# One-hots by scalar comparisons, weighted one-hots on ScalarE, and chunks in pairs on TensorE in a graph kernel's first pass

## The chip, the cores and the metric

The kernel runs on one core of a Trainium2 chip. The metric is the device time of one execution in microseconds, the median of the timed runs.

## What is computed

A graph has 6250 nodes with 256 features (`x`) and 106250 edges (`src`, `dst`, `edge_weight`), sorted by destination. Four layers follow one another; each adds its result to `x` and takes a layer norm.

```python
# layer 0: attention over heads for the first 6250 edges (the gathers of x by src and dst)
x = layernorm(x + attention(x, src[:n], dst[:n], W0, attn_l, attn_r))
# layer 1: plain graph convolution
norm = d1[src] * d1[dst];            x = layernorm(x + segment_sum((x @ W1)[src] * norm, dst))
# layer 2: two weighted convolutions with self loops, bias and relu
norm = d2[row] * w * d2[col];        h = relu(segment_sum(norm * (x @ W2)[row], col) + b1)
                                     h = relu(segment_sum(norm * (h @ W3)[row], col) + b2);  x = layernorm(x + h)
# layer 3: convolution the other way round (sums over src), with self loops
vals = d3[src] * d3[dst];            x = layernorm(x + segment_sum(vals * (x @ W4.T)[dst], src))
```

## The kernel before

**Blocks and chunks.** The nodes are cut into NBK = 49 blocks of 128. The edges of a destination block stand in NC = 18 chunks of 128 edges (882 chunks in all). For one chunk GpSimd gathers 128 table rows from memory into a slot of `G` (7 slots, L1766), VectorE makes a 128x128 one-hot `M` of the destinations by a scalar comparison (4 buffers, `onehot`, L1041 without weights, L1043 with), and TensorE multiplies the two in f32 and adds up the block in PSUM (L1689). Pass one (layer 1) does this for all 882 chunks. In it ScalarE also writes the edge weight as a 257th column of the slot (`weight_column`, L1362), three chunks ahead.

**What is built behind pass one.** Passes two and three do the last ND = 17 blocks (32 to 48, called dense here) from a matrix of weights that lies ready in memory (`AW`), and pass four (layer 3) is a product with the whole adjacency matrix (`AT`). Both are built during pass one, one source block after another in the order `BORDER`, in which a dense one comes at every third place or so. A function `build_steps` gives each step a due time in chunks, PITCH = 17 chunks a block; `behind` hands each engine its own steps, and each engine does those of chunk k after its own part of chunk k. Every engine works strictly in its order.

**The steps of block i.** VectorE marks the cell of each edge (`cellhot`), TensorE counts ranks (`rank`, L1577 and L1579), VectorE picks the rank and makes slot numbers (`pick`, `pack`, `over`, `less`, `slots`, L1094 to L1114), multiplies the cell one-hots by what is carried (`load`, L1122 and L1123, into `OHP`), and compares all 18 columns of slot numbers with a table in one instruction (`place`, L1126, into `S`). TensorE moves the payload to its slot by 18 products (`permute`, L1589). ScalarE copies the outcome out of PSUM as bf16 (`cells`, L1372, into `clb`: source, destination, and for dense blocks three pieces of the weight). Then 26 positions are done in batches of CB = 2: VectorE compares destinations (`doh`, L1139) and sources (`soh`, L1140, 128x512) for two positions at once, and for dense blocks multiplies the first by the three weight pieces (`wdoh`, L1143). TensorE multiplies them (`pair`, L1601; `weigh`, L1612, six products a position). ScalarE copies each pair of positions out of PSUM (`keep`, L1379; `keepw`, L1386), and SyncE stores them.

**Waits around the change.** `place` makes the whole of `S` and needs all permutes of the block before to be done; `permute` waits for it and for `load`. `pairhot` waits for the cells and for the batch four back to be used. `weigh` waits for VectorE's `wdoh`. A chunk's product on TensorE waits for the gather, for `M` and for the weight column (`s_wc`); the gather waits for a slot (7 chunks back).

Of the kernel before, what the change touches and what calls it, by code (L numbers as in the profile page):

```python
# [43 lines left out]
FILL_B, FILL_C = 1840, 600  # L44
# [149 lines left out]
def build_steps():  # L194
# [27 lines left out]
    V_.append((PITCH * NBK, ("bad",)))  # L222
# [288 lines left out]
def program(nc, a, out):  # L511
# [5 lines left out]
    with ExitStack() as ctx:  # L517
# [75 lines left out]
        irep18 = sb("irep18", [P, P, NC], BF16)  # L593
        irep25 = sb("irep25", [P, NPR, NC], BF16)
        irepS, irepD = sb("irepS", [P, D, CB], BF16), sb("irepD", [P, P, CB], BF16)
# [3 lines left out]
        S = sb("S", [P, P, NC], BF16)  # L599
        soh = [sb(f"soh{i}", [P, D, CB], BF16) for i in range(NB)]  # L600
        doh = [sb(f"doh{i}", [P, P, CB], BF16) for i in range(NB)]
        atp = [sb(f"atp{i}", [P, 512], BF16) for i in range(4)]
        wdoh = [sb(f"wdoh{i}", [P, 3, P, CB], BF16) for i in range(NB)]
# [8 lines left out]
        slots, slotb = sb("slots", [P, NBK, NC]), [sb(f"slotb{i}", [P, NC], BF16) for i in range(2)]  # L612
        clb = [sb(f"clb{i}", [P, 5, NPOS], BF16) for i in range(2)]
# [39 lines left out]
        s_wg, s_kw, s_wc, s_dn, s_lo, s_hi = (sem(n_) for n_ in ("s_wg", "s_kw", "s_wc", "s_dn", "s_lo", "s_hi"))  # L653
# [86 lines left out]
        def vector(e):  # L740
# [316 lines left out]
            def behind_(step):  # L1057
# [17 lines left out]
                elif kind == "cellhot":  # L1075
                    O_ = OH[j]
                    if i == 0:
                        w.wait_ge(s_io, 8)
                        w.wait_ge(s_ev, project_of(1, NBK - 1) + 1)
                        after("cell", "pay1", "dsum", "d1")  # L1080
# [27 lines left out]
                elif kind == "slots":  # L1108
                    if i >= 2:
                        after(("place", i - 2))  # L1110
                    done(e.scalar_tensor_tensor(out=slots[:, b, :], in0=OH[j][:, own + 1, :], scalar=-128.0, in1=slot0[:, :],
                                                op0=ALU.mult, op1=ALU.add), ("slots", i))
                    after(("slots", i))
                    done(e.tensor_copy(slotb[j][:, :], slots[:, b, :]), ("slotb", i))  # L1114
# [9 lines left out]
                elif kind == "place":  # L1124
                    after(("slotb", i))
                    done(e.tensor_tensor(S[:, :, :], irep18[:, :, :], slotb[j][:, :].unsqueeze(1).to_broadcast([P, P, NC]),  # L1126
                                         ALU.is_equal), ("place", i))
                elif kind == "pairhot":
# [3 lines left out]
                    value = lambda q, m_: clb[j][:, q, j0:j0 + g].unsqueeze(1).to_broadcast([P, m_, g])  # L1132
# [6 lines left out]
                    done(e.tensor_tensor(doh[n_ % NB][:, :, 0:g], irepD[:, :, 0:g], value(1, P), ALU.is_equal), ("doh", n_))  # L1139
                    done(e.tensor_tensor(soh[n_ % NB][:, :, 0:g], irepS[:, :, 0:g], value(0, D), ALU.is_equal), ("pairhot", n_))  # L1140
                    if b >= NB0:
                        after(("doh", n_))
                        done(e.tensor_tensor(wdoh[n_ % NB][:, :, :, 0:g], doh[n_ % NB][:, :, 0:g].unsqueeze(1).to_broadcast([P, 3, P, g]),  # L1143
                                             clb[j][:, 2:5, j0:j0 + g].unsqueeze(2).to_broadcast([P, 3, P, g]), ALU.mult), ("weighted", n_))
                elif kind == "bad":
                    after(("place", NBK - 1))
# [15 lines left out]
                elif kind == "deg":  # L1162
                    if b == 0:
                        w.wait_ge(s_io, 9)
# [90 lines left out]
        def scalar(e):  # L1255
# [108 lines left out]
            def behind_(step):  # L1364
                if step[0] == "cells":
# [3 lines left out]
                    if i >= 2:  # L1369
                        n_ = NBT * (i - 1) - 1  # L1370
                        w.wait_ge(s_v, max(at["pairhot", n_], at.get(("weighted", n_), 0)))
                    e.copy(clb[i % 2][:, 0:q_, :].rearrange("p k t -> p (k t)"), PC[:, 0:q_ * NPOS]).then_inc(s_ce, 1)  # L1372
# [73 lines left out]
        def tensor(e):  # L1446
# [115 lines left out]
            def behind_(step):  # L1562
# [20 lines left out]
                elif kind == "permute":  # L1583
                    c = step[2]
                    q_ = 5 if b >= NB0 else 2
                    w.wait_ge(s_v, at["place", i])
                    w.wait_ge(s_v, at["load", i])
                    w.wait_ge(s_ce, i)
                    e.matmul(PC[:, 0:q_ * NPOS], S[:, :, c], OHP[:, 0:q_, :, c], start=c == 0, stop=c == NC - 1).then_inc(s_pm, 1)  # L1589
                elif kind == "pair":  # L1590
# [5 lines left out]
                    d_, s_ = doh[n_ % NB][:, :, q], soh[n_ % NB][:, :, q]  # L1596
# [6 lines left out]
                elif kind == "weigh":  # L1603
# [4 lines left out]
                    w.wait_ge(s_v, at["weighted", n_])  # L1608
                    fill_free(w, "keepw", i, pair // 2)
                    for h in range(2):  # L1610
                        for t in range(3):
                            ins = e.matmul(ps[:, h * P:(h + 1) * P], soh[n_ % NB][:, h * P:(h + 1) * P, q], wdoh[n_ % NB][:, t, :, q],  # L1612
# [49 lines left out]
            def aggregate(p):  # L1662
                other = behind(p, 2)
                end = chunks_of(p)
                for k in range(end):
# [24 lines left out]
                    for step in other[k]:  # L1690
                        behind_(step)
                    for step in due(FOLLOW[p][2], k, end):
                        follow(p, step)
# [31 lines left out]
        def gpsimd(e):  # L1725
# [27 lines left out]
            io(irep18[:, :, :], [[1, P], [0, NC]])  # L1753
            io(irepS[:, :, :], [[1, D], [0, CB]])
# [163 lines left out]
```

## Time and profile before

| | us |
|---|---|
| median of 3 timed runs (3676.34 to 3695.49) | 3684.63 |
| the profiled execution, its own time | 3691.6 |
| its span | 3689.8 |

The profile is of one execution. Its page gives for each engine the time in which it was busy: PE is TensorE, DVE VectorE, ACT ScalarE, POOL GpSimd. Pass one runs from 294.8 us (first `M`) to about 1572 us, pass two to about 2340, pass three to about 3118, pass four to the end. A group of instructions is shown as busy time, mean ns of one, and the idle time of its engine just before them with what ended it. Instructions of one engine overlap a little, so a mean is somewhat longer than the distance from one start to the next.

### The profile page before, as it was taken

The page shows a single profiled execution, that of the slowest core. Times are in us where ns is not written, and L with a number is a line of the kernel's source. Part 1 is how long each engine was busy: PE and PEld are TensorE (multiplying, and loading weights), DVE is VectorE, ACT ScalarE, POOL GpSimd, SP SyncE. Part 2 cuts the span into 40 slices and gives each one's busy share as a digit, 9 for nine tenths or more (in the row PEclk, how much of TensorE's full clock was granted, in tenths as well). Part 3 has the DMA queues.
Part 4 walks back from the last instruction along what each step waited for, and adds up shares of the span by engine and source line. Part 5 has one row for each costly group of instructions (what it writes and reads, how often), then busy time and mean ns, then how long its engine had stood idle before and what let it go on. Part 6 is the DMA issues. An engine that isn't in the chain of part 4 may idle for free.

```text
span 3689.8 us, 53868 instructions
## 1 busy us (share of the span) xinstructions
PE 3322.1 (90%) x18533; PEld 2696.9 (73%) x18533; DVE 1899.0 (51%) x6309; ACT 1079.3 (29%) x2821; POOL 2223.8 (60%) x2148
## 2 busy tenths in 40 slices
PE   6667888888889888799999999699999998999999
PEld 5644666666666666578888888588888886888887
DVE  7665777777777777634444434233333333333333
ACT  3353454554445555400000000001111111322232
POOL 7505777777777777767777777477777775000000
PEclk9788999999999999999999999799999999999999
DMA  6123666776667676656555555556666654444443
GB/s 196 54 103 119 198 215 208 215 222 199 201 204 229 206 220 210 199 181 178 175 176 179 179 175 177 188 176 180 184 180 180 184 180 150 145 164 154 160 151 116
DMA packets 323660, 655.95 MB, mean 178 GB/s; under 512 B 63162, under 2 KB 186262, under 8 KB 323388
## 3 DMA queue, kind: packets, MB, share of 16 engines
q1 hardware_dynamic: 218732, 369.66, 29.9%
q0 software_dynamic: 102720, 280.94, 27.2%
q8 instruction: 157, 2.57, 0.3%
q10 hardware_dynamic: 1936, 1.84, 0.2%
q14 instruction: 115, 0.94, 0.1%
HBM read 484.19 MB, written 168.01 MB: 177 GB/s over the span
## 4 chain that ended last, share of the span: by engine, by line
PE 66%; DMA 13%; DVE 8%; POOL 7%; issue 4%; ACT 2%; SPq 0%; DVEq 0%; ACTq 0%
PE PS L1689 18%; PE PS L1651 16%; PE PS L1711 14%; DMA G<-T,idx 10%; POOL G L1766 7%; PE PS L1612 2%; PE PS L1630 2%; PE PS L1480 2%; PE PS L1579 2%; PE PS L1481 2%; PE PS L1601 2%; PE PS L1589 2%; DMA G<-in_x,srcN 1%; DVE soh L1140 1%; PE PS L1457 1%
## 5 line engine op out<-in xcount | busy, mean ns | idle before, releaser
L1766 POOL DMA_INDIRECT G<-T,idx x2034 | 2105.2, 1035 | 829.9 <-issue 423.7
L1689 PE MATMUL PS<-G,M 128*128 128x256 f32 (+1 forms) x4068 | 1286.7, 399 | 194.9 <-DMA G<-T,idx 131.7
L1689 PEld LDWEIGHTS PS<-G,M 128*128 128x128 f32 x4068 | 723.6, 194 | 385.5 <-issue 79.8
L1651 PE MATMUL PS<-H,aw 128*128 128x256 f32 x3332 | 913.8, 382 | 6.6 <-DMA aw<-AW 6.6
L1043 DVE TENSOR_SCALAR M<-iot,dlo,wD 128x128 f32<-128x128 f32 x1152 | 414.4, 367 | 723.4 <-PE PS L1689 720.2
L1651 PEld LDWEIGHTS PS<-H,aw 128*128 128x128 f32 x3332 | 623.9, 191 | 85.5 <-issue 7.3
L1711 PE MATMUL PS<-HH,cr 128*128 128x512 f32 x2401 | 548.6, 391 | 7.7 <-DVE cr L1208 7.6
L1711 PEld LDWEIGHTS PS<-HH,cr 128*128 128x128 f32 x2401 | 452.1, 189 | 104.6 <-issue 8.2
L1379 ACT CAST atp<-PS 128x512 bf16<-128x512 f32 (+1 forms) x637 | 363.7, 571 | 400.2 <-PE PS L1601 395.4
L1601 PE MATMUL PS<-soh,doh 128*128 128x256 bf16 x1225 | 282.4, 285 | 1.7 <-ACT awp L1386 1.5
L1041 DVE TENSOR_SCALAR M<-iot,dlo 128x128 f32<-128x128 f32 x882 | 251.5, 293 | 62.0 <-PE PS L1689 61.4
L1140 DVE TENSOR_TENSOR soh<-irepS,clb 128x512 bf16<-128x512 bf16 x637 | 266.5, 418 | 0.0
L1208 DVE CAST cr<-br 128x3584 fp32r<-128x3584 bf16 (+1 forms) x46 | 87.9, 1910 | 313.0 <-PE PS L1711 234.5
L1589 PE MATMUL PS<-OHP,S 128*128 128x52 bf16 (+1 forms) x882 | 237.0, 309 | 6.2 <-DVE S L1126 6.2
L1415 ACT CAST cr<-br 128x3584 fp32r<-128x3584 bf16 (+1 forms) x45 | 136.8, 3040 | 341.9 <-PE PS L1711 315.6
L1139 DVE TENSOR_TENSOR doh<-irepD,clb 128x256 bf16<-128x256 bf16 x637 | 182.1, 286 | 99.2 <-ACT clb L1372 89.2
L1274 ACT COPY xT<-PS 128x256 f32<-128x256 f32 x294 | 107.5, 374 | 395.5 <-PE PS L1458 393.6
L1612 PEld LDWEIGHTS PS<-wdoh,soh 128*128 128x128 bf16 x2652 | 179.0, 98 | 43.4 <-issue 1.7
L1612 PE MATMUL PS<-wdoh,soh 128*128 128x128 bf16 x2652 | 202.4, 220 | 0.0
L1362 ACT COPY G<-wD 128x1 f32<-128x1 f32 x882 | 160.3, 194 | 41.1 <-PE PS L1689 40.9
L1304 ACT ACTIVATE X<-X,nmr,rq 128x256 f32<-128x256 f32 x196 | 112.6, 599 | 183.8 <-DVE nmr L1031 168.8
L1386 ACT COPY awp<-PS 128x512 f32<-128x512 f32 (+1 forms) x221 | 126.0, 570 | 129.5 <-PE PS L1612 108.1
(218 smaller groups left out, 3064.6 us busy)
## 6 DMA issues: line engine op xcount, KB each, us to landing
aw<-AW SPq DMA_DIRECT2D x238, 448.0 KB, 3.6
AT<-atp SPq DMA_DIRECT2D x588, 128.0 KB
br<-AT SPq DMA_DIRECT2D x84, 896.0 KB, 4.7
AW<-awp SPq DMA_DIRECT2D x204, 256.0 KB
G<-T,idx POOLq DMA_INDIRECT x2034
T<-H SPq DMA_DIRECT2D x96, 128.0 KB
X<-in_x SPq DMA_DIRECT2D x8, 768.0 KB, 15.0
T<-tst SPq DMA_DIRECT2D x48, 128.0 KB, 3.1
```

Source lines behind the costliest of these rows:

```text
L1041: ins = e.tensor_scalar(M[m % NM][:, :], iot[:, :], dlo[:, b, c:c + 1], None, ALU.is_equal)
L1043: ins = e.tensor_scalar(M[m % NM][:, :], iot[:, :], dlo[:, b, c:c + 1], wD[:, b, c:c + 1], ALU.is_equal, ALU.mult)
L1139: done(e.tensor_tensor(doh[n_ % NB][:, :, 0:g], irepD[:, :, 0:g], value(1, P), ALU.is_equal), ("doh", n_))
L1140: done(e.tensor_tensor(soh[n_ % NB][:, :, 0:g], irepS[:, :, 0:g], value(0, D), ALU.is_equal), ("pairhot", n_))
L1379: e.copy(atp[n_ % 4][:, 0:wid], fill_bank(*step)[:, 0:wid]).then_inc(s_ar, 1)
L1589: e.matmul(PC[:, 0:q_ * NPOS], S[:, :, c], OHP[:, 0:q_, :, c], start=c == 0, stop=c == NC - 1).then_inc(s_pm, 1)
L1601: ins = e.matmul(ps, d_, s_, start=j != own + 1, stop=True)
L1612: ins = e.matmul(ps[:, h * P:(h + 1) * P], soh[n_ % NB][:, h * P:(h + 1) * P, q], wdoh[n_ % NB][:, t, :, q], start=j != own + 1 and h == 0 ...
L1651: ins = e.matmul(ps, aw[n_ % NAW][:, s_ % 7, :], H[:, s_, :], start=False, stop=s_ == NBK - 1)
L1689: e.matmul(ps, M[m % NM][:, :], G[slot][:, 0:wide_], start=p == 1 and c == 0, stop=c == NC - 1).then_inc(s_mm, 1)
L1711: ins = e.matmul(SET[g % 2][s % 4][:, :], cr[j % 2][:, bb, (s % 4) * P:(s % 4 + 1) * P], HH[:, :, b, :], start=b == 0, stop=b == NBK - 1)
L1766: e.indirect_dma_start(G[slot][:, 0:D], None, TAB[p][0:N, :], bass.IndirectOffsetOnAxis(ap=idx[:, k // NC, k % NC:k % NC + 1], axis=0)).th ...
```

## The change

- `S` is laid out by column (`[P, NC, P]`), and `place` becomes 18 steps, one a column: a scalar comparison of a row of counts (`iob`) with the f32 slot numbers. Each is due one chunk ahead of its permute and waits for that column's permute of the block before. The bf16 copy of the slot numbers goes. The permutes are spread over 15 chunks instead of 14, and `cells` and the pairs move by one chunk.
- `soh` is laid out by position, and each position's sources are compared by a scalar comparison of 128x256, two a batch. `cells` therefore writes two copies: f32 (`clf`, all values) and bf16 (`clb`, destinations only).
- The weighted one-hots of dense blocks are made by ScalarE: three activations a position, a copy of `doh` with a scale per partition, counted by a new semaphore `s_ws`, for which `weigh` waits.
- In pass one TensorE does the products of two chunks, then the steps behind both.

```diff
@@ build_steps
-               (k + 8, ("slots", i)), (k + PITCH - 1, ("load", i)), (k + PITCH - 1, ("place", i))]
+               (k + 8, ("slots", i)), (k + PITCH - 1, ("load", i))]
         for c in range(NC):
-            T_.append((k + c * 14 // NC, ("permute", i, c)))
-        S_.append((k + 14, ("cells", i)))
-        k += 15
+            V_.append((k - 1 + c * 15 // NC, ("place", i, c)))
+            T_.append((k + c * 15 // NC, ("permute", i, c)))
+        S_.append((k + 15, ("cells", i)))
+        k += 16
...
             if b >= NB0:
+                S_.append((at_ + 1, ("weighted", i, j)))
                 T_.append((at_ + 2, ("weigh", i, j)))
@@ vector: behind_
                 elif kind == "slots":
-                    if i >= 2:
-                        after(("place", i - 2))
                     done(e.scalar_tensor_tensor(out=slots[:, b, :], ...), ("slots", i))
-                    after(("slots", i))
-                    done(e.tensor_copy(slotb[j][:, :], slots[:, b, :]), ("slotb", i))
...
                 elif kind == "place":
-                    after(("slotb", i))
-                    done(e.tensor_tensor(S[:, :, :], irep18[:, :, :], slotb[j][:, :].unsqueeze(1).to_broadcast([P, P, NC]),
-                                         ALU.is_equal), ("place", i))
+                    c = step[2]
+                    after(("slots", i))
+                    w.wait_ge(s_pm, NC * (i - 1) + c + 1)
+                    done(e.tensor_scalar(S[:, c, :], iob[:, 0:P], slots[:, b, c:c + 1], None, ALU.is_equal), ("place", i, c))
...
-                    done(e.tensor_tensor(soh[n_ % NB][:, :, 0:g], irepS[:, :, 0:g], value(0, D), ALU.is_equal), ("pairhot", n_))
-                    if b >= NB0:
-                        after(("doh", n_))
-                        done(e.tensor_tensor(wdoh[n_ % NB][:, :, :, 0:g], doh[n_ % NB][:, :, 0:g].unsqueeze(1).to_broadcast([P, 3, P, g]),
-                                             clb[j][:, 2:5, j0:j0 + g].unsqueeze(2).to_broadcast([P, 3, P, g]), ALU.mult), ("weighted", n_))
+                    for q in range(g):
+                        done(e.tensor_scalar(soh[n_ % NB][:, q, :], iob[:, :], clf[j][:, 0, j0 + q:j0 + q + 1], None, ALU.is_equal),
+                             ("pairhot", n_))
@@ scalar: behind_
-                    e.copy(clb[i % 2][:, 0:q_, :].rearrange("p k t -> p (k t)"), PC[:, 0:q_ * NPOS]).then_inc(s_ce, 1)
+                    e.copy(clf[i % 2][:, 0:q_, :].rearrange("p k t -> p (k t)"), PC[:, 0:q_ * NPOS])
+                    e.copy(clb[i % 2][:, :], PC[:, NPOS:2 * NPOS]).then_inc(s_ce, 1)
+                elif step[0] == "weighted":
+                    i, j = step[1], step[2]
+                    n_, q = NBT * i + j // CB, j % CB
+                    w.wait_ge(s_v, at["doh", n_])
+                    w.wait_ge(s_ce, i + 1)
+                    for t in range(3):
+                        ins = e.activation(wdoh[n_ % NB][:, q, t, :], doh[n_ % NB][:, :, q], ACT.Copy, scale=clf[i % 2][:, 2 + t, j:j + 1])
+                    ins.then_inc(s_ws, 1)
@@ tensor: weigh
-                    w.wait_ge(s_v, at["weighted", n_])
+                    w.wait_ge(s_ws, weighed_before(i) * NPOS + j + 1)
@@ tensor: aggregate
-                for k in range(end):
+                def chunk(k):
...
+                run = 2 if p == 1 else 1
+                for k0 in range(0, end, run):
+                    for k in range(k0, k0 + run):
+                        chunk(k)
+                    for k in range(k0, k0 + run):
+                        for step in other[k]:
+                            behind_(step)
+                        for step in due(FOLLOW[p][2], k, end):
+                            follow(p, step)
```

## Rows read from the trace of the kernel before

**Rows 1.** The page: span, and busy time of each engine over it.
```profile
span 3689.8 us, 53868 instructions
PE 3322.1 (90%) x18533; PEld 2696.9 (73%) x18533; DVE 1899.0 (51%) x6309; ACT 1079.3 (29%) x2821; POOL 2223.8 (60%) x2148
```

**Rows 2.** Stretches: length, busy PE PEld DVE ACT POOL (count), granted clock, DMA share, GB/s.
```profile
294.80:1572.00 1277.20, 1106.20 (x7808) 814.94 (x7809) 929.80 (x3516) 631.41 (x1991) 995.50 (x882) 0.96 0.67 204
1572.00:2340.00 768.00, 756.78 (x3987) 666.13 (x3986) 310.12 (x842) 59.59 (x145) 551.75 (x565) 1.00 0.59 177
```

**Rows 3.** Groups of instructions, 374 to 1560 us: the gathers of pass one.
```profile
L1766 POOL DMA_INDIRECT G<-T,idx x822 | 936.2, 1139 | 251.3 <-issue 181.6 <-PE PS L1689 69.6
```

**Rows 4.** Timeline of GpSimd: start, us, instruction, idle before and releaser.
```profile
1063.40 0.94 POOL L1766 DMA_INDIRECT G<-T,idx  x1 [0.30 <-issue]
1066.15 3.38 POOL L1766 DMA_INDIRECT G<-T,idx  x1 [0.30 <-PE PS L1689]
```

**Rows 5.** Timeline of VectorE beside the long gather.
```profile
1066.00 0.89 DVE L1122 TENSOR_TENSOR OHP<-payw,OH 128x1404 bf16<-128x1404 bf16 x1
1066.80 0.64 DVE L1123 TENSOR_TENSOR OHP<-pay,OH 128x936 bf16<-128x936 bf16 x1
1067.36 1.35 DVE L1126 TENSOR_TENSOR S<-irep,slotb 128x2304 bf16<-128x2304 bf16 x1
```

**Rows 6.** Busy time: 17 dense stretches (two, sum), 32 others (one, sum).
```profile
444.20:473.30 29.10, 26.24 (x224) 21.00 (x223) 22.45 (x80) 15.32 (x44) 23.00 (x20) 0.88 0.69 220
939.40:968.90 29.50, 25.01 (x227) 19.65 (x226) 22.50 (x80) 15.70 (x45) 23.43 (x20) 1.00 0.70 219
...
sum 474.10, PE 422.07 PEld 335.09 DVE 378.71 ACT 263.19 POOL 375.26; mean PE 24.83 PEld 19.71 DVE 22.28 ACT 15.48 POOL 22.07
...
1063.00:1089.80 26.80, 21.83 (x103) 14.09 (x103) 16.98 (x68) 10.27 (x35) 21.01 (x20) 0.89 0.56 163
...
sum 729.00, PE 634.35 PEld 450.58 DVE 526.70 ACT 351.92 POOL 573.21; mean PE 19.82 PEld 14.08 DVE 16.46 ACT 11.00 POOL 17.91
```

**Rows 7.** ScalarE: groups by shape, whole span, and one place of its timeline.
```profile
L1379 ACT CAST atp<-PS 128x512 bf16<-128x512 f32 x588 | 345.4, 588 | 387.0 <-PE PS L1601 382.3 <-issue 0.4 <-DMA AT<-atp 0.3
L1274 ACT COPY xT<-PS 128x256 f32<-128x256 f32 x294 | 107.5, 374 | 395.5 <-PE PS L1458 393.6 <-issue 1.4
L1300 ACT ACTIVATE tst<-PS,d 128x256 f32<-128x256 f32 x49 | 23.2, 474 | 138.2 <-PE PS L1481 138.2
L1326 ACT ACTIVATE hb<-hb 128x256 f32<-128x256 f32 x49 | 20.4, 416 | 449.4 <-DVE hb L1003 449.4
L1379 ACT CAST atp<-PS 128x256 bf16<-128x256 f32 x49 | 18.4, 375 | 13.2 <-PE PS L1601 13.1
...
923.15 0.60 ACT L1304 ACTIVATE X<-X,nmr,rq 128x256 f32<-128x256 f32 x1
923.66 0.17 ACT L1362 COPY G<-wD 128x1 f32<-128x1 f32 x1
```

**Rows 8.** VectorE: groups by shape, whole span.
```profile
L1043 DVE TENSOR_SCALAR M<-iot,dlo,wD 128x128 f32<-128x128 f32 x1152 | 414.4, 367 | 723.4 <-PE PS L1689 720.2
L1140 DVE TENSOR_TENSOR soh<-irepS,clb 128x512 bf16<-128x512 bf16 x637 | 266.5, 418 | 0.0
L1041 DVE TENSOR_SCALAR M<-iot,dlo 128x128 f32<-128x128 f32 x882 | 251.5, 293 | 62.0 <-PE PS L1689 61.4
L1139 DVE TENSOR_TENSOR doh<-irepD,clb 128x256 bf16<-128x256 bf16 x637 | 182.1, 286 | 99.2 <-ACT clb L1372 89.2 <-PE PS L1612 6.3 <-issue 1.9
L1143 DVE TENSOR_TENSOR wdoh<-doh,clb 128x768 bf16<-128x768 bf16 x221 | 121.9, 552 | 0.0
L1094 DVE TENSOR_TENSOR sel<-PS,OH 128x468 f32<-128x468 f32 x49 | 31.6, 646 | 136.4 <-PE PS L1579 131.6 <-issue 4.8
L1025 DVE TENSOR_SCALAR q<-mv 128x1 f32<-128x1 f32 x98 | 14.4, 149 | 0.1
```

**Rows 9.** Groups of instructions, 1600 to 2340 us: the gathers of pass two.
```profile
L1766 POOL DMA_INDIRECT G<-T,idx x554 | 541.0, 977 | 199.8 <-issue 117.4 <-PE PS L1689 82.5
```

More of the change, by code:

```diff
@@ L43 @@
 NAW = 5
-FILL_B, FILL_C = 1840, 600
+FILL_B, FILL_C = 3120, 472
 class Lane:
@@ L598, in program @@
         sel, slot0 = sb("sel", [P, NPOS, NC]), sb("slot0", [P, NC])
-        S = sb("S", [P, P, NC], BF16)
-        soh = [sb(f"soh{i}", [P, D, CB], BF16) for i in range(NB)]
+        S = sb("S", [P, NC, P], BF16)
+        soh = [sb(f"soh{i}", [P, CB, D], BF16) for i in range(NB)]
         doh = [sb(f"doh{i}", [P, P, CB], BF16) for i in range(NB)]
         atp = [sb(f"atp{i}", [P, 512], BF16) for i in range(4)]
-        wdoh = [sb(f"wdoh{i}", [P, 3, P, CB], BF16) for i in range(NB)]
+        wdoh = [sb(f"wdoh{i}", [P, CB, 3, P], BF16) for i in range(NB)]
         awp = [sb(f"awp{i}", [P, 512]) for i in range(3)]
@@ L611, in program @@
         sb = tiles(passes)
-        slots, slotb = sb("slots", [P, NBK, NC]), [sb(f"slotb{i}", [P, NC], BF16) for i in range(2)]
-        clb = [sb(f"clb{i}", [P, 5, NPOS], BF16) for i in range(2)]
+        slots = sb("slots", [P, NBK, NC])
+        clb = [sb(f"clb{i}", [P, NPOS], BF16) for i in range(2)]
+        clf = [sb(f"clf{i}", [P, 5, NPOS]) for i in range(2)]
         pay2, payw = sb("pay2", [P, NBK, 2, NC], BF16), sb("payw", [P, ND, 3, NC], BF16)
@@ L652, in program @@
         s_rk, s_pm, s_ce, s_pc, s_ar = sem("s_rk"), sem("s_pm"), sem("s_ce"), sem("s_pc"), sem("s_ar")
-        s_wg, s_kw, s_wc, s_dn, s_lo, s_hi = (sem(n_) for n_ in ("s_wg", "s_kw", "s_wc", "s_dn", "s_lo", "s_hi"))
+        s_wg, s_ws, s_kw, s_wc, s_dn, s_lo, s_hi = (sem(n_) for n_ in ("s_wg", "s_ws", "s_kw", "s_wc", "s_dn", "s_lo", "s_hi"))
         s_ap, s_wp = [sem(f"s_ap{i}") for i in range(4)], [sem(f"s_wp{i}") for i in range(3)]
@@ L1138, in behind_ @@
                             w.wait_ge(s_wg, batch_end(before) - NPOS * (before // NBT - weighed_before(before // NBT)))
[L1139 to L1144 removed]
+                    done(e.tensor_tensor(doh[n_ % NB][:, :, 0:g], irepD[:, :, 0:g], clb[j][:, j0:j0 + g].unsqueeze(1).to_broadcast([P, P, g]),
+                                         ALU.is_equal), ("doh", n_))
+                    for q in range(g):
+                        done(e.tensor_scalar(soh[n_ % NB][:, q, :], iob[:, :], clf[j][:, 0, j0 + q:j0 + q + 1], None, ALU.is_equal),
+                             ("pairhot", n_))
                 elif kind == "bad":
[L1146 removed]
+                    after(("place", NBK - 1, NC - 1))
                     done(e.tensor_scalar(slots[:, :, :], slots[:, :, :], 127.5, 0.0, ALU.is_ge, ALU.add, accum_out=bad[:, :]), "bad")
@@ L1585, in behind_ @@
                     q_ = 5 if b >= NB0 else 2
-                    w.wait_ge(s_v, at["place", i])
-                    w.wait_ge(s_v, at["load", i])
+                    w.wait_ge(s_v, max(at["place", i, c], at["load", i]))
                     w.wait_ge(s_ce, i)
-                    e.matmul(PC[:, 0:q_ * NPOS], S[:, :, c], OHP[:, 0:q_, :, c], start=c == 0, stop=c == NC - 1).then_inc(s_pm, 1)
+                    e.matmul(PC[:, 0:q_ * NPOS], S[:, c, :], OHP[:, 0:q_, :, c], start=c == 0, stop=c == NC - 1).then_inc(s_pm, 1)
                 elif kind == "pair":
@@ L1595, in behind_ @@
                     fill_free(w, "keep", i, pair // 2)
-                    d_, s_ = doh[n_ % NB][:, :, q], soh[n_ % NB][:, :, q]
+                    d_, s_ = doh[n_ % NB][:, :, q], soh[n_ % NB][:, q, :]
                     if j == own:
@@ L1611, in behind_ @@
                         for t in range(3):
-                            ins = e.matmul(ps[:, h * P:(h + 1) * P], soh[n_ % NB][:, h * P:(h + 1) * P, q], wdoh[n_ % NB][:, t, :, q],
+                            ins = e.matmul(ps[:, h * P:(h + 1) * P], soh[n_ % NB][:, q, h * P:(h + 1) * P], wdoh[n_ % NB][:, q, t, :],
                                            start=j != own + 1 and h == 0 and t == 0, stop=t == 2, skip_group_check=True)
@@ L1689, in aggregate @@
                     e.matmul(ps, M[m % NM][:, :], G[slot][:, 0:wide_], start=p == 1 and c == 0, stop=c == NC - 1).then_inc(s_mm, 1)
[L1690 to L1693, printed above, removed]
+                run = 2 if p == 1 else 1
[7 more added lines that the diff above has]
+                            follow(p, step)
                 for step in due(FOLLOW[p][2], end, end):
```

19 lines of the change are left out of this document (9 added, 10 removed).

## The prediction

> **What bounds the kernel now.** I read the page first, then pass one by stretches [rows 2], then each engine's rows inside it. The span is 3689.8 us, the profiled execution took 3691.6 and the median of the timed runs is 3684.63, so the sum below is made against 3691.6 and 7 us come off at the end [rows 1]. TensorE is the busiest engine over the whole, but the change touches pass one only: 294.8 to 1572.0 us, 1277 us for 882 gathered chunks, 1.45 us a chunk. There TensorE is busy 1106 us, VectorE 930, ScalarE 631 [rows 2].
>
> GpSimd's row decides. In 1186 us of pass one it issues 822 gathers, mean 1139 ns, and the idle time ahead of them is 251.3 us, 0.31 us each: 936.2 + 251.3 = 1187.5, the whole window [rows 3]. The timeline shows the same 0.30 us ahead of every gather, whoever is named as releaser, and 0.94 to 0.95 us for most [rows 4]. So a chunk can't take less than 1.25 us, 882 of them 1103 us; the rest (some 170 us) is gathers that are stretched. The gather of 3.38 us at 1066.15 lies under the two OHP products and the S comparison of VectorE [rows 4, 5]. GpSimd therefore sets the mean pace; TensorE, at 87% of the stage, is close behind.
>
> Then I cut pass one into the 17 stretches in which the pair steps of a dense block (one of blocks 32 to 48, with "weigh" steps) run and the 32 of other blocks, 17 chunks each. Dense: 474.1 us, 27.9 each, TensorE 24.8, VectorE 22.3, ScalarE 15.5. Others: 729.0 us, 22.8 each, TensorE 19.8, VectorE 16.5, ScalarE 11.0 [rows 6]. The reader is to see that ScalarE has 12.4 us to spare in a dense stretch and no more, and that VectorE has 6.3 in another.
>
> **The change part by part.**
>
> *Weighted one-hots to ScalarE.* VectorE loses 13 products of mean 552 ns a dense block, of which 0.47 is its own time (the next instruction starts about 0.08 before an end, as 1066.00, 1066.80, 1067.36 show) [rows 5, 8]: 6.1 us. ScalarE gains 3 x 26 = 78 activations of 128x128, bf16 from SBUF, with a scale per partition. No row has one. Nearest: the relu of 128x256 from and to SBUF without such a scale, 416 ns; the activation of 128x256 from PSUM with a scale, 474, against 374 for the copy of the same tile, so a scale costs 100 ns; 512 columns 588 against 375 for 256, so 0.83 ns a column and 106 for 128 [rows 7]. From relu: 416 - 106 + 100 = 410; from the scaled one: 474 - 106 = 368. ScalarE's next instruction starts about 0.09 to 0.10 us before the end of the one ahead (923.15 + 0.60 against 923.66) [rows 7]. That leaves 0.27 to 0.31; I take 0.30, the side that reads SBUF. 78 x 0.30 = 23.4 us. Bounds: 0.17 if the scale is free and SBUF is as near as PSUM (374 - 106 - 100), 13.1 us; 0.41 with no overlap at all, 32 us.
>
> Now ScalarE in a dense stretch: 15.5 + 23.4 + 0.1 for the second copy of the cells = 39.0 us, for 27.9 that the stretch takes. This can't be spread over the neighbours, though ScalarE is idle half of the stage: its queue is in order, the weight column of chunk k+3 is issued in the same queue, and TensorE waits for it (s_wc) before chunk k. So TensorE is never more than 3 chunks past ScalarE, the slots of G come free by TensorE, and the gathers stop with it. A start ahead of 3 chunks at most is paid back at the other end. I add 0.7 us for copies out of PSUM whose pair isn't ready: its 12.4 us of idle time there are nearly all waits for TensorE's pairs [rows 7], and go once it is itself the late one. 39.7 - 27.9 = 11.8 us, times 17 = **+200 us**. Bounds: 28.7 us a stretch (+14 us in all) and 47.6 (+335). What lies behind ScalarE then: the weight column, so chunk matmul, so VectorE's one-hot M (4 buffers) and the gathers; all idle, none pays again. TensorE's clock may be granted lower there (it was 0.88 to 1.00 in such stretches at 85 to 90% busy [rows 6]); 24.8 us of work even twice as slow in part stays under 39.7, so I put it at nothing.
>
> *Source one-hots by scalar comparison.* Each pair batch loses one 128x512 comparison (418 ns, 0.34 own) and gains two of 128x256: 13 x 0.34 = 4.4 us out, 26 in. Nearest rows: M, a scalar comparison of 128x128 f32, 293 ns; the doh comparison of 256 bf16, 286; a tensor_scalar of 128x1, 149 [rows 8]. Bounds 0.18 and 0.41 each, 0.10 and 0.33 own; I take the doh row, 0.20 own: 5.2 us.
>
> *Slots by scalar comparison.* One S of 1353 ns (1.27 own) and one cast of 0.09 go, 18 comparisons of 128x128 bf16 come, 0.07 (128x1) to 0.20 own (M's row), taken 0.16: 2.9 us in, 1.36 out. They go one by one ahead of their permute steps, each after the permute of the block before; those are 17 chunks old, so the wait is free. The last "place" is now due 14 chunks later and the cells one chunk later; this moves the tail of the build by one chunk, 1.3 us, hidden in the 13 chunks of pass one after it.
>
> VectorE in another stretch: 16.5 - 5.8 + 8.1 = 18.8 us (bounds 14.6 and 22.9), in a dense one 22.3 - 6.1 - 5.8 + 8.1 = 18.5, far below ScalarE. At 18.8 it stays below the gathers' 17 x 1.25 = 21.3, but closely: its waits in order (for the rank sums and for the cells, 136 and 99 us over 49 blocks, 4.8 a block [rows 8]) must shrink. What is won: no 1.3 us burst over a gather, so up to 1.3 us a block. I take 0.5 us, since VectorE is nearly full: 32 x 0.5 = **-16 us** (bounds -1.5 x 32 = -48, and the rival below). In dense stretches it is worth nothing.
>
> A rule of the Trainium skill speaks against these two. The slow gathers stand over tensor_tensor work [rows 4, 5], while the gathers of pass two, with one scalar comparison (M, 367 ns) beside each, have mean 977 ns, 0.03 over the shortest [rows 8, 9]. The Trainium skill (SBUF — State Buffer, section Who interferes with whom) says that tensor_scalar in a two-port mode takes the port pair that GpSimd needs to write descriptors and blocks it for the whole instruction, while tensor_tensor contends only with GpSimd's reads. By that rule 44 new short comparisons a block could each hold a gather; by the row they cost 44 x 0.03 = 1.3 us a block, what S gives back. The row I follow.
>
> *Two chunks in a row on TensorE.* The second chunk's matmul now stands ahead of the first one's steps. Its M and its weight column are issued before those steps on their engines, so nothing locks; but TensorE waits for the later gather with both chunks' steps behind it. At 2.5 us of gathers a pair and 2 x 19.8/17 = 2.3 us of TensorE work [rows 6] this just fits. Bounds: -20 us (fewer changes between f32 and bf16 operands; in 441 pairs 0.05 each) and +0.1 us a chunk in the 32 stretches, +54. Taken: 0. The fill sizes only move addresses.
>
> Sum: 3691.6 + 200 - 16 = 3875.6; minus 7: **3868 us**.
>
> **The rivals.**
>
> *VectorE late as well.* If the bf16 comparisons cost their upper bounds, VectorE needs 22.9 us in the 32 others and keeps half of its waits, 2.4: 25.3 against 22.8, +80 us instead of -16. For it: M's row is slow for its size. Against: bf16 rows (286 ns for 256 columns) are quick. Gathers blocked by the rule above end in the same place. 3868 + 96 = 3964 us.
>
> *ScalarE keeps up, and the change is faster.* The deciding point is (27.9 - 15.5) / 78 = 0.16 us for one weighted copy. At or under it the dense stretches are let go by VectorE (22.3 to 18.5) and lose their stretched gathers: 27.9 to some 26, -32 us; the others lose 0.8 each, -26: 3627 us. For it: 106 ns of columns and a 128x1 copy that ScalarE gets through in 0.10. Against: the scale's 100 ns in the one row that has it, and SBUF reads that are slower, not faster (416 against 374).
>
> *About even.* A weighted copy of 0.17 to 0.18, or 0.2 with more gain elsewhere: +14 to +34 against -16 to -48, 3685 us.
>
> *The pairing alone hurts.* TensorE waits at each pair for a gather that isn't there: +54 us on the forecast, 3922, inside the range.
>
> **How the numbers follow.** Forecast 0.70, VectorE late too 0.10, pairing hurts 0.06, ScalarE keeps up 0.10, even 0.04. Outside of +-0.5% (18 us, what a measurement of this kernel can tell from no change): slower 0.86, same 0.04, faster 0.10. The range for 8 in 10 goes from 3745 (a copy at 0.22: 15.6 + 17.2 = 32.8 and 4.9 x 17 = +83, -16) to 3970 (a copy at 0.34 and 42.8 us, +253, or VectorE late).
>
> **What would show it.** Right: the 17 dense stretches at 39 to 40 us with ScalarE busy over 95% and TensorE near 60%; weighted copies near 0.40 us long, starting 0.30 apart; chunk matmuls waiting for the weight column, the weigh matmuls for the weighted copies; GpSimd with gaps over 0.30 us there; others at 22 to 23 us with no gather over 2.5 us but under the OHP products. Wrong: weighted copies less than 0.16 apart, dense stretches under 30 us, or others above 25 us with VectorE full. Passes two, three and four are to be unchanged within 2 us each.

## The result and the profile after

| | before, us | after, us |
|---|---|---|
| median of 4 timed runs | 3686.43 | 3798.61 |
| profiled execution, its span | 3689.8 | 3797.7 |
| pass one, first to last `M` | 294.8 to 1568.7 | 303.2 to 1676.8 |
| what follows it | 2121.1 | 2120.9 |

The ratio is 1.03, with a 95% interval of 1.028 to 1.032: slower by 112 us, for 184 forecast. In the profiled executions pass one grew by 99.7 us; 8.4 us more lie ahead of its first `M`; the passes behind are unchanged, as forecast.

The busy times over pass one and over all that follows it, in the profile after; the first row answers to that of pass one in [rows 2]. The columns are start and end, length, busy time of TensorE, its weight loads, VectorE, ScalarE and GpSimd, granted clock, DMA share, GB/s.

```profile
303.20:1680.00 1376.80, 1132.71 (x7806) 797.32 (x7807) 938.70 (x4716) 979.05 (x3366) 866.25 (x882) 0.96 0.62 189
1680.00:3797.00 2117.00, 2025.75 (x9668) 1727.17 (x9667) 779.62 (x2251) 315.14 (x463) 1113.17 (x1153) 0.99 0.55 170
```

ScalarE's busy time rose from 631 to 979 us, which is still only 71% of the pass. The average hides the cause. Cut from the first weighted copy of a dense block to its last, the pass shows 17 phases; three of them and the sum:

```profile
385.00:421.40 36.40, 28.28 (x252) 20.96 (x250) 17.91 (x90) 36.40 (x124) 18.20 (x19) 0.95 0.63 198
...
922.30:960.40 38.10, 30.40 (x254) 22.47 (x255) 19.90 (x101) 37.26 (x126) 19.58 (x21) 0.91 0.62 198
1002.00:1038.90 36.90, 27.78 (x254) 20.23 (x255) 19.93 (x101) 36.90 (x126) 20.07 (x21) 1.00 0.66 206
...
sum 627.60, PE 484.23 PEld 355.23 DVE 322.62 ACT 625.49 POOL 338.85; mean PE 28.48 PEld 20.90 DVE 18.98 ACT 36.79 POOL 19.93
```

ScalarE is busy for 625.5 of 627.6 us. TensorE is at 77% (near 60% was forecast), VectorE at 51%. The 17 dense stretches of the kernel before took 474.1 us [rows 6]. The groups of ScalarE inside the phase of 36.9 us at 1002, with no idle time ahead of any:

```profile
L1379 ACT ACTIVATE wdoh<-doh,clf 128x128 bf16<-128x128 bf16 x78 | 25.4, 438 | 0.0
L1387 ACT CAST atp<-PS 128x512 bf16<-128x512 f32 (+1 forms) x13 | 7.9, 606 | 0.0
L1394 ACT COPY awp<-PS 128x512 f32<-128x512 f32 x12 | 7.6, 629 | 0.0
L1361 ACT COPY G<-wD 128x1 f32<-128x1 f32 x17 | 3.9, 229 | 0.0
```

78 copies, 17 weight columns, 13 and 12 copies out of PSUM: one block's work for 17 chunks. The instructions overlap, so these busy times add up to more than the phase. What one copy takes of the queue is read from one start to the next:

```profile
1004.31 1.87 ACT L1379 ACTIVATE wdoh<-doh,clf 128x128 bf16<-128x128 bf16 x6
1006.07 0.18 ACT L1361 COPY G<-wD 128x1 f32<-128x1 f32 x1
```

Six copies in 1.76 us are 0.29 each; over all 1326 the mean is 0.295. TensorE meets ScalarE's lateness at the `weigh` products (L1619), and in its order everything behind them comes late. It waits there for the weighted copies, and for copies out of PSUM (374 to 1560 us: total, times, longest):

```profile
PEld PS L1619 <- ACT wdoh L1379: 148.5, 227, 1.4
PE PS L1619 <- ACT wdoh L1379: 63.3, 115, 1.1
PE PS L1619 <- ACT atp L1387: 37.3, 43, 1.2
```

The weight column, for which the prediction had the chunk products wait, holds them for 2.8 us in the whole execution (10.3 in the kernel before).

The chain of waits over the whole (share of the span by line) now names lines of ScalarE that it didn't have; ScalarE has 15% of it:

```profile
PE 58%; ACT 15%; DVE 12%; DMA 7%; issue 4%; POOL 3%; SPq 0%; ACTq 0%; DVEq 0%; POOLq 0%
PE PS L1658 16%; PE PS L1696 15%; PE PS L1725 14%; ACT wdoh L1379 9%; DMA G<-T,idx 5%; POOL G L1779 2%; DVE soh L1142 2%; ACT atp L1387 2%; PE PS L1637 2%; ACT awp L1394 2%; PE PS L1488 2%; PE PS L1587 2%; PE PS L1489 2%; DVE M L1043 1%; DVE S L1128 1%
```

GpSimd is no longer the pace of these phases. The gathers from 374 to 1560 us, which answer to [rows 3]: shorter by 154 ns each, and with waits for TensorE's chunk products in place of a gap of 0.30 everywhere.

```profile
L1779 POOL DMA_INDIRECT G<-T,idx x756 | 744.4, 985 | 443.0 <-PE PS L1696 294.4 <-issue 148.6
```

The new and changed instructions, from the page (busy in all, mean ns):

```profile
L1379 ACT ACTIVATE wdoh<-doh,clf 128x128 bf16<-128x128 bf16 x1326 | 429.0, 426 | 0.0
L1142 DVE TENSOR_SCALAR soh<-iob,clf 128x256 bf16<-128x256 bf16 x1274 | 307.9, 290 | 0.0
L1128 DVE TENSOR_SCALAR S<-iob,slots 128x128 bf16<-128x128 bf16 x882 | 212.9, 256 | 0.0
```

### The profile page after: what moved, and what is told of

Read it like the earlier page. It is cut to its first block, busy times and chain, and to the rows that moved or that the text cites. A ratio compares the mean times of both kernels' runs of the same rounds, so it can differ in the third digit from the quotient of the medians.

```text
span 3797.7 us, 56498 instructions
## 1 busy us (share of the span) xinstructions
PE 3351.7 (88%) x18533; PEld 2682.4 (71%) x18533; DVE 1909.2 (50%) x7509; ACT 1427.6 (38%) x4196; POOL 2089.3 (55%) x2147
## 4 chain that ended last, share of the span: by engine, by line
PE 58%; ACT 15%; DVE 12%; DMA 7%; issue 4%; POOL 3%; SPq 0%; ACTq 0%; DVEq 0%; POOLq 0%
PE PS L1658 16%; PE PS L1696 15%; PE PS L1725 14%; ACT wdoh L1379 9%; DMA G<-T,idx 5%; POOL G L1779 2%; DVE soh L1142 2%; ACT atp L1387 2%; PE PS L1637 2%; ACT awp L1394 2%; PE PS L1488 2%; PE PS L1587 2%; PE PS L1489 2%; DVE M L1043 1%; DVE S L1128 1%
## 5 line engine op out<-in xcount | busy, mean ns | idle before, releaser
L1779 POOL DMA_INDIRECT G<-T,idx x2034 | 1977.5, 972 | 1071.4 <-PE PS L1696 495.6
L1696 PE MATMUL PS<-G,M 128*128 128x256 f32 (+1 forms) x4068 | 1228.3, 396 | 142.4 <-DMA G<-T,idx 62.6
L1696 PEld LDWEIGHTS PS<-G,M 128*128 128x128 f32 x4068 | 737.6, 193 | 340.0 <-DVE M L1043 139.2
L1658 PEld LDWEIGHTS PS<-H,aw 128*128 128x128 f32 x3332 | 623.2, 191 | 85.2 <-issue 7.3
L1379 ACT ACTIVATE wdoh<-doh,clf 128x128 bf16<-128x128 bf16 x1326 | 429.0, 426 | 0.0
L1619 PE MATMUL PS<-wdoh,soh 128*128 128x128 bf16 x2652 | 224.3, 225 | 115.2 <-ACT wdoh L1379 69.9
L1142 DVE TENSOR_SCALAR soh<-iob,clf 128x256 bf16<-128x256 bf16 x1274 | 307.9, 290 | 0.0
L1619 PEld LDWEIGHTS PS<-wdoh,soh 128*128 128x128 bf16 x2652 | 167.9, 101 | 194.2 <-ACT wdoh L1379 164.9
L1608 PE MATMUL PS<-soh,doh 128*128 128x256 bf16 x1225 | 274.3, 281 | 16.9 <-ACT awp L1394 7.3
L1128 DVE TENSOR_SCALAR S<-iob,slots 128x128 bf16<-128x128 bf16 x882 | 212.9, 256 | 0.0
L1325 ACT ACTIVATE hb<-hb 128x256 f32<-128x256 f32 x49 | 20.4, 416 | 450.1 <-DVE hb L1005 450.1
```

Source lines behind the costliest of these rows:

```text
L1128: done(e.tensor_scalar(S[:, c, :], iob[:, 0:P], slots[:, b, c:c + 1], None, ALU.is_equal), ("place", i, c))
L1142: done(e.tensor_scalar(soh[n_ % NB][:, q, :], iob[:, :], clf[j][:, 0, j0 + q:j0 + q + 1], None, ALU.is_equal), ("pairhot", n_))
L1379: ins = e.activation(wdoh[n_ % NB][:, q, t, :], doh[n_ % NB][:, :, q], ACT.Copy, scale=clf[i % 2][:, 2 + t, j:j + 1])
L1608: ins = e.matmul(ps, d_, s_, start=j != own + 1, stop=True)
L1619: ins = e.matmul(ps[:, h * P:(h + 1) * P], soh[n_ % NB][:, q, h * P:(h + 1) * P], wdoh[n_ % NB][:, q, t, :], start=j != own + 1 and h == 0 ...
L1658: ins = e.matmul(ps, aw[n_ % NAW][:, s_ % 7, :], H[:, s_, :], start=False, stop=s_ == NBK - 1)
```

## The experiments

Theory 1 was that of the prediction: ScalarE full in the dense phases is the loss, and shorter holds on the gathers are the gain. The other theories and rivals are named where an expectation uses them. The first four kernels undo parts of the change (kernel before: 3690.86 us); the next four do one part alone (kernel before: 3684.79 us). Every profile is of one execution, so a few us between two of them say little.

**The weighted one-hots back on VectorE.**

```diff
-                S_.append((at_ + 1, ("weighted", i, j)))
...
+                    if b >= NB0:
+                        after(("doh", n_))
+                        done(e.tensor_tensor(wdoh[n_ % NB][:, :, :, 0:g], doh[n_ % NB][:, :, 0:g].unsqueeze(1).to_broadcast([P, 3, P, g]),
+                                             clb[j][:, 2:5, j0:j0 + g].unsqueeze(2).to_broadcast([P, 3, P, g]), ALU.mult), ("weighted", n_))
```

> The changed kernel with one part undone: the weighted one-hots are made by VectorE again, as one product of 128x768 a batch; the comparisons by scalars and the chunks in pairs stay. Theory 1 (ScalarE, full for 36.9 us in each of 17 dense blocks, costs some 172 us, and the comparisons by scalars give back some 70 because no long comparison holds a gather): pass one comes to 1200 us or less and the time to 3690 - 70 = 3620 us, within 25. Rival 2 (VectorE only looked relieved because ScalarE held everything back; with the product back it is full at 18.8 + 6.1 = 25 us of 27 in a dense block and behind in the others): 3680 to 3730 us.

Measured 3637.03 us (before 3690.86; ratio 0.9863, 0.9834 to 0.9893). With this one part undone, the change is a gain of 54 us. 3637 against 3799 puts the part at 162 us. Rival 2 falls.

**One of three pieces on ScalarE.**

```diff
-                    for t in range(3):
-                        ins = e.activation(wdoh[n_ % NB][:, q, t, :], doh[n_ % NB][:, :, q], ACT.Copy, scale=clf[i % 2][:, 2 + t, j:j + 1])
+                    ins = e.activation(wact[n_ % NB][:, q, :], doh[n_ % NB][:, :, q], ACT.Copy, scale=clf[i % 2][:, 2, j:j + 1])
```

> The changed kernel with only the first of the three weighted pieces on ScalarE (26 activations a dense block instead of 78); VectorE makes the other two in one product of 128x512 a batch. Theory 1: ScalarE needs 15.5 + 26 x 0.32 = 23.8 us in a dense block and is under the 25 to 27 us that the block takes anyway, so the loss is gone at once and the time is that of the kernel with all three on VectorE, within 15 us (about 3620). Rival 3 (it is not ScalarE's amount of work but the new hand-over from VectorE over ScalarE to TensorE, which stays here): at least half of the 172 us stay, 3700 us or more.

Measured 3633.65 us (0.9855, 0.9823 to 0.9887), level with none on ScalarE. The hand-over from VectorE over ScalarE to TensorE is in place here and no cost of it shows; rival 3 falls. The 17 phases, cut in the same way at the first and last such copy (sum row):

```profile
sum 461.40, PE 426.07 PEld 354.27 DVE 377.04 ACT 380.92 POOL 344.12; mean PE 25.06 PEld 20.84 DVE 22.18 ACT 22.41 POOL 20.24
```

The reader is to see 461.4 us where the changed kernel has 627.6: 166 us apart, which is all of the 165 us between the two kernels. ScalarE is busy 22.4 of 27.1 us here, and no longer decides.

**Without the pairs, and the scalar comparisons alone.** Both have `run = 1` in `aggregate`, so TensorE does the steps of each chunk behind that chunk; the second has the weighted one-hots on VectorE too.

> The changed kernel with one part undone: TensorE does the steps of each chunk behind that chunk again, not behind two. Theory 1: no part in the loss and none in the gain, 3799 within 10 us. Rival 4 (the pairs gain by fewer changes between f32 and bf16 operands, or let TensorE run past a late step): 3820 us or more. Rival 5 (the pairs hurt, since TensorE waits for the second gather): 3785 us or less.

Measured 3779.09 us (1.0243, 1.0211 to 1.0275): 20 us better than the changed kernel. Theory 1's zero was wrong here, rival 5's sign right, and rival 4, by which the pairs gain, falls.

> The changed kernel with the weighted one-hots on VectorE again and without the pairs; only the comparisons by scalars are left of the change. Theory 1: as the kernel with only the weighted one-hots put back, within 10 us. Rival 4: 15 us or more above it, since here ScalarE hides nothing. Rival 5: 15 us or more below it.

Measured 3613.64 us (0.9798, 0.9769 to 0.9828), 23 us under the one with pairs. This is the best on this chip: two of the four edits without the other two, 77 us faster than before. GpSimd has its gap of 0.3 us ahead of each gather here too (252.1 us over 822). The same 822 gathers as in [rows 3] (here 374 to 1473 us), and then the whole of pass one:

```profile
L1782 POOL DMA_INDIRECT G<-T,idx x822 | 848.2, 1032 | 252.1 <-issue 186.6 <-PE PS L1699 65.6
```

```profile
295.80:1480.40 1184.60, 1068.89 (x7799) 775.98 (x7799) 1032.71 (x4937) 635.67 (x2039) 904.18 (x881) 0.98 0.72 219
```

These gathers are 88 us shorter than before (936.2), 107 ns each, with the same idle time (251.3); they took 87 us less from the first to the last, and pass one is 90 us shorter. The gathers' length accounts for the gain. VectorE isn't relieved: its busy time rose from 929.8 to 1032.7 us.

**The weighted one-hots on ScalarE alone.** The kernel before, with the activations in place of L1143.

> The kernel before with one part of the change alone: the weighted one-hots by ScalarE, with an f32 copy of the cells of dense blocks for the scales. Theory 1: 17 phases of 36.9 us with ScalarE full, for some 26.8 us that their chunks took: +172 us, 3855 to 3870 us, less up to 20 because VectorE's product no longer holds gathers in the neighbouring stretches. Rival 3 (the weighted copies cost only together with the scalar comparisons): 3780 us or less.

Measured 3806.75 us (before 3684.79; 1.033, 1.0311 to 1.0348), +122 us. Slower as theory 1 says, but by 50 less. Its phases sum to 630.3 us with ScalarE busy 623.2, much as in the changed kernel:

```profile
sum 630.30, PE 486.84 PEld 351.57 DVE 282.88 ACT 623.17 POOL 378.78; mean PE 28.64 PEld 20.68 DVE 16.64 ACT 36.66 POOL 22.28
```

Pass one grew by less than the phases did: 1386.9 us for 1273.8, +113, where the phases have +156 over the 474.1 of before. Some 43 us come back outside of them; the prediction had no such term. Cut at VectorE's first `doh` of each block instead, the 17 stretches right behind a dense one show it: 311.5 us for 365.3.

Four kernels without pairs show that the parts don't simply add (us):

| weighted one-hots | comparisons as before | comparisons by scalars |
|---|---|---|
| on VectorE | 3691 and 3685 (kernel before, two groups) | 3614 |
| on ScalarE | 3807 | 3779 |

The weighted one-hots on ScalarE cost 122 us in the left column and 165 in the right; the comparisons gain 77 (or 71) in the upper row and 28 in the lower. The traces, cut at the first `doh` too, tell where. In the 17 dense stretches the comparisons save 33 us where ScalarE has room (470.1 to 436.7) and none where it is full (631.2 and 633.2): a stretched gather costs nothing while ScalarE holds everything back. In the 32 others they save 56 and 31. Why it is less there too is open.

**The slots by scalars alone.** L1126 as 18 comparisons, with their due times.

> The kernel before with one part of the change alone: 18 comparisons of 128x128 by scalars in place of the one of 128x2304, with their due times. Theory 1 (the one long comparison holds a gather for 1.3 us in each of 49 blocks, and TensorE's permutes wait for it): the gathers over 2 us go down to the OHP products' 1.5 to 2.5 us, -40 to -64 us, about 3635. Rival 2 (VectorE's own time grows by 1.5 us a block or more and is what counts): no gain, 3680 or more.

Measured 3665.18 us (0.9944, 0.9924 to 0.9965), -20 us, half of what was expected. The longest gather fell from 4.01 to 2.03 us, and the mean of the same 822 from 1139 to 1097 ns:

```profile
L1763 POOL DMA_INDIRECT G<-T,idx x2034: 940/946/2034, 313.7 to 3090.9; - x185
L1763 POOL DMA_INDIRECT G<-T,idx x822 | 901.8, 1097 | 251.7 <-issue 175.8 <-PE PS L1686 75.8
```

**The sources by scalars alone.** `soh` as in the change, L1126 as before.

> The kernel before with one part of the change alone: two comparisons of 128x256 by scalars in place of one of 128x512, and a second copy of the cells by ScalarE. Theory 1: VectorE's own time is about even (2 x 0.24 against 0.34 would be +1.8 us a block), less of it holds gathers: between -20 and +10 us, 3675. Rival 2: VectorE later by 13 x 0.1 us a block, +30 us or more. Rival of the Trainium skill (SBUF - State Buffer, Who interferes with whom): scalar comparisons in a two-port mode block the gathers, whose mean in pass one would rise over 1139 ns.

Measured 3654.46 us (0.9921, 0.9902 to 0.9939), -30 us, beyond the range that theory 1 gave. This is the test of the port rule that the prediction weighed. The Trainium skill (SBUF — State Buffer, Who interferes with whom) says that scalar comparisons in a two-port mode block GpSimd's descriptor writing for the whole instruction. With 1274 more of them the gathers became shorter, mean 1085 ns:

```profile
L1770 POOL DMA_INDIRECT G<-T,idx x822 | 892.1, 1085 | 252.3 <-issue 180.7 <-PE PS L1693 71.6
```

The comparison costs 290 ns for 256 columns and 256 for 128, 0.27 ns a column, half of the 0.52 of tensor_tensor ((418 - 286) / 256, [rows 8]). The Trainium skill (VectorE: DVE Perf Modes, Mode 4×_2P — both tricks at once) has four elements a cycle with both ports only; at its clock of 0.96 GHz that is an estimate of 0.26 ns a column, so the rule ought to apply. Yet two such comparisons hold the gathers less than the one of 418 ns that they replace. The measurement decides against the rule as a price, for comparisons as short as these. The trace of the kernel with the comparisons alone gives a price: 40 of its gathers (374 to 1470 us) lie over more than 250 ns of them and over no `tensor_tensor` of two tiles in SBUF. Their mean is 985 ns and the longest took 1109. In the kernel before, the 197 gathers of that window over no such `tensor_tensor` have a mean of 946.

The two parts alone give 50 us of the 77 that they give together; 6 us of the rest lie between the two groups' values for the kernel before. The same 822 gathers took 34 and 43 us less with one part, 87 with both.

**The pairs alone.**

> The kernel before with one part of the change alone: TensorE does two chunks of pass one, then the steps behind both. Theory 1: nothing, within 10 us of the kernel before. Rival 4: -15 us or more. Rival 5: +15 us or more, with chunk products waiting longer for their gathers.

Measured 3706.23 us (1.0049, 1.0032 to 1.0066), +21 us, about the amount that the pairs cost with all else in place. But it doesn't lie in the same place. Of the 16.7 us between the profiled executions (3706.5, 3689.8), 6.1 lie ahead of pass one, 5.0 in it and 5.6 behind it, where nothing was changed. With the comparisons in place the pairs lengthen pass one by 26 us (1184.2 to 1210.3), and with everything in place by 18 (1355.3 to 1373.6). GpSimd's rows show it, this kernel and then the one with the comparisons and pairs (374 to 1565 and to 1499 us):

```profile
L1772 POOL DMA_INDIRECT G<-T,idx x822 | 933.5, 1136 | 259.2 <-issue 173.0 <-PE PS L1689 86.2
L1782 POOL DMA_INDIRECT G<-T,idx x822 | 847.6, 1031 | 278.7 <-issue 182.9 <-PE PS L1699 95.7
```

The gathers are as long as without pairs, but wait longer for a slot, that is for TensorE's chunk products: 86.2 us for 69.6 [rows 3], and 95.7 for 65.6. In the second case the growth of idle time, 26.6 us, is the whole of pass one's growth. So the pairs make TensorE late. The cause that rival 5 names, TensorE waiting for a later gather, is not what makes it so. From 374 to 1560 us TensorE waits less for gathers than before (62.5 for 82.4 us) and more for the one-hots `M`, on weight loads and matmuls:

```profile
PEld PS L1689 <- DVE M L1041: 96.0, 112, 3.1
PE PS L1689 <- DMA G<-T,idx: 62.5, 79, 3.1
PE PS L1689 <- DVE M L1041: 44.1, 68, 2.7
```

The kernel before has 36.9 and 5.2 us there. VectorE issues the `M` of chunk k+1 ahead of its steps of chunk k, so behind those of k-1. Without pairs TensorE has its own steps of chunk k to do before it needs that `M`; with pairs it needs it at once. That is theory 6. It explains where TensorE waits, not the amount: the waits for `M` grow by 98 us here and pass one by 5.

**The last four, on another chip.** They ran where the kernel before took 4067.41 us. Only differences within this group are read.

> The changed kernel with two of the three weighted pieces on ScalarE (52 activations a dense block), the third by VectorE. Theory 1, ScalarE full: its phase of 36.9 us shrinks by 26 x 0.32 to 28.6 us, for some 25 us that the same chunks take where ScalarE doesn't decide: 17 x 3.6 = 61 us over the kernels with one piece or none (3634, 3637), about 3695 us. A rival in which each hand-over costs alike would lie half way between 3634 and 3799, at 3717 or above, and one piece should not have been free.

Measured 4113.12 us (ratio 1.0109, 1.0069 to 1.0149): 65 us above the kernel with early one-hots and pairs below, 55 above the one with one piece and no pairs. Neither differs from it by the second piece alone: against the first it lacks the early one-hots, against the second it has pairs. If each of these is worth the 20 us that pairs cost on the first chip, the second piece costs 35 to 45 us, an estimate. The 61 expected are neither met nor refuted. The 82 us of the rival with equal hand-overs are more than any of these. Its 17 phases take 33.9 us in the mean, with ScalarE busy 29.6 of them (87%, over 90% in four); with one piece and no pairs they take 30.5, with ScalarE busy 22.6. The 3.4 us between them, times 17, are 58 us, so the loss lies in the phases. But it is there before ScalarE is full: the phase of 28.6 us that theory 1 expected was not reached. One of the fullest:

```profile
1074.30:1105.70 31.40, 27.73 (x253) 21.33 (x251) 20.57 (x103) 29.37 (x100) 18.23 (x20) 0.93 0.71 218
```

**One-hots M two chunks ahead**, with and without pairs:

```diff
-                onehot(p, 0)
+                ahead = 2 if p == 1 else 1
...
-                    if k + 1 < end:
-                        onehot(p, k + 1)
+                    if k + ahead < end:
+                        onehot(p, k + ahead)
```

> The changed kernel with the weighted one-hots on VectorE (3637 us) and VectorE's one-hot M in pass one issued two chunks ahead instead of one. Theory 6: the pairs cost 20 us because the second product of a pair needs an M that VectorE issues only behind its steps of the chunk before the pair; with M earlier the waits for M (147 + 73 us) fall by more than half and the time comes to that of the kernel without pairs, 3614, or below. Rival 5 (the pairs cost by later gathers and slots): 3630 us or more.

> The kernel with only the comparisons by scalars (weighted one-hots on VectorE, no pairs, 3614 us) and M two chunks ahead in pass one. Theory 6: little is left to win, since without pairs the waits for M are 56 + 19 us and the gathers set the pace: 3600 to 3614 us.

Measured 4048.10 (0.9933, 0.9906 to 0.996) and 4046.98 us (0.9949, 0.9929 to 0.9969). In the first, the chunk products wait for `M` 10.2 us in pass one, where the kernel without early one-hots has 216 on the first chip (374 to 1700 and to 1500 us):

```profile
PEld PS L1701 <- DVE M L1042: 6.1, 6, 2.4
PE PS L1701 <- DVE M L1042: 4.1, 4, 2.0
```

With early one-hots pairs and no pairs are level, as theory 6 wants. But pairs without early one-hots have no run on this chip, so that the 20 us of the pairs come back isn't shown. Part of the wait moved, too: the `pair` products wait 113.0 us for VectorE's source one-hots here, and 4.1 in the kernel of the 216. The expected absolute times can't be checked.

> The comparisons by scalars, one weighted piece of three on ScalarE, two on VectorE, no pairs. Theory 1: ScalarE stays under the block's own time (23.8 us), VectorE is relieved by 13 x 0.13 us a dense block: 3605 to 3615 us, the best so far or equal to it.

Measured 4057.86 us (0.9966, 0.9946 to 0.9987), 10 to 11 us above the two with early one-hots. Whether it would match 3614 us on the first chip is open.

## Why the prediction was right, point by point

**What bounds the kernel.** Right, and it carried the rest: with the comparisons alone 822 gathers are 88 us shorter, and they took 87 us less from the first to the last.

**Weighted one-hots on ScalarE, +200 us forecast.** The core of the mechanism was right: ScalarE in order, full in each of 17 dense phases, GpSimd and VectorE with idle time behind it. Undoing the part gives 162 to 165 us, and one piece instead of three shortens the phases from 627.6 to 461.4 us, 166.

The path was wrong in one link. The prediction had chunk products wait for the weight column, and named that as a sign; they wait 2.8 us for it. The `weigh` products wait for the weighted copies instead, as it also said, and TensorE's own order does the rest. The sum doesn't use which of the two it is.

The size of a phase was 39.7 us in the forecast and 36.9 in the trace. Over the 17 phases, by start to next start, a copy takes 0.295 us, so 78 take 23.0 us (23.4 forecast). The old work takes 13.7 us with both copies of the cells, for 15.6: the 15.5 were busy time, in which an instruction that stands alone counts the end that a full queue overlaps, and I had taken that overlap off the new instructions only. Idle time is 0.1 us for the 0.7 that were added. With 36.9 us, 9.0 x 17 = +153.

The term that the sum lacked is what comes back outside of the phases. With this part alone the phases grow by 156 us, pass one by 113 and the time by 122. "This can't be spread over the neighbours" was too strict: some 43 us of it came back there.

**Scalar comparisons, -16 us forecast.** Right in sign, too small: -77 us where ScalarE has room (-20 and -30 alone), -28 where it is full, which is the case that was forecast. That they are worth nothing in dense stretches held there (631.2 and 633.2 us). The 32 others take 21.1 us each in the changed kernel (676.7 in all), for 22 to 23 forecast. The durations were forecast well (290 ns for 256 columns, forecast 286; 256 for 128 columns, forecast 240), but I let VectorE's own load eat the gain. It doesn't, since VectorE's waits shrink: for the rank sums and the cells from 122 and 84 us to 38 and 38 between 374 and 1560 us, with the comparisons alone. And I counted only the long S comparison, while the 637 comparisons of 128x512 held gathers as well (-30 us alone).

**Pairs, 0 forecast.** Wrong: +20 to +23 us in each of three comparisons (3799 to 3779, 3637 to 3614, 3706 to 3685), inside the bounds of -20 to +54. In two of the three the loss lies in pass one, where GpSimd has more idle time ahead of its gathers. TensorE didn't wait longer for gathers, as the upper bound had it, but for `M`; that this wait is the whole cost isn't shown. The gain of the lower bound, from fewer changes between f32 and bf16 operands, shows in no time.

**The sum.** Taken from the two traces, the change is +153.5 us in the dense phases (forecast +200), -54 in the rest of pass one (799.7 to 746.0; forecast -16) and +8.4 ahead of it (forecast 0), 108 in all. The stretches of before and the phases of after aren't cut at quite the same places; cut at the first `doh` in both, the terms are +155 (470.1 to 625.0) and -53 (729.5 to 676.7). The forecast of 3868 was 70 high because the loss was set too high and the gain too low; the pairs, set too low, took some 20 us of that error back, which was luck. By the runs, in the order of the prediction, the parts are +122, -28 and +20; from the other side they are -77, +23 and +162. Each order adds up, and neither is the one true share of a part. Of the rivals, ScalarE keeping up (0.16 us a copy needed, 0.295 measured) and VectorE late as well are both refuted; the pairs did hurt, but on top of a smaller sum.

The 8 us ahead of pass one are not assigned. The first `M` starts at 294.8 to 297.2 us in six kernels of this chip and at 300.8 to 303.2 in four: the changed one, the one without pairs, the one with pairs alone and the one with the slots alone. No edit is common to these four.

## What to carry to other kernels

An engine at half load over a stage may have no room where the work would go: cut the stage into the stretches that get the new instructions, and count them there. Take the old work of a queue at its start-to-start time, not at its busy time, before you ask whether it fits. And where one engine sets the pace, look at what stretches its instructions: splitting one VectorE comparison of 1.35 us and halving others made the gathers, not VectorE, faster. Where two edits touch the same limit, measure them together and apart: each of them had two prices here, by what else stood in the kernel.

## What the runs showed of the hardware

- Gathers issued by GpSimd are stretched while VectorE compares or multiplies two bf16 tiles of SBUF without a pause: up to 4.01 us for 0.94. With scalar comparisons in place of most of them the longest is 1.72 us in the changed kernel and 2.17 with the comparisons alone.
- One scalar comparison of 256 bf16 columns takes 290 ns, of 128 columns 256, two in a row of 256 columns 0.47 us.
- A copy of 128x128 bf16 by ScalarE from SBUF, with a scale per partition, lasts 426 ns in a full queue and holds it for 0.295 us. In the same queue ScalarE's old work of a dense block took 13.7 us, where it had shown 15.5 us busy with pauses between.
- A second chip ran the same kernel in 4067 us for 3686. Single instructions lasted about as long there in other kernels of this case (median 280 ns for the one-hot of a chunk against 275 to 279, 587 against 586 for the copy out of PSUM), and a window of 500 us in pass four has TensorE busy for all of it on both. But passes two to four took 2331 us for 2121, and GpSimd's idle time ahead of a gather in pass one, 0.31 us in the kernel with the comparisons alone on the first chip, was 0.55 in the same kernel with early one-hots (464.2 us over 842 gathers), 0.29 of it waits for TensorE's chunk products. The cause is open.
